# Attention scores kept unscaled in the eviction, the row's step moved into the exponential

## The chip, the cores and the metric

The kernel runs on one core of one Trainium2 chip. The metric is the device time of one execution in microseconds (us). TensorE multiplies matrices into PSUM, VectorE (DVE) and ScalarE (ACT) work element by element, GpSimd (POOL) does casts and issues some DMAs, SyncE (SP) issues the others.

## The reference, cut to what matters

One layer of a perceiver: cross-attention with rounded operands, then self-attention, then a mixture of experts. The change lies in the cross-attention alone. There, 4096 query rows attend to 8192 context rows in 16 heads of 16 channels:

```
q = x @ Wq + bq ; k, v = split(cond @ Wkv + bkv)          # q also times 1/sqrt(16)
q = fq_sym(q, axis=-1)      # s = max|q|/127 per row and head; round(q/s) * s
k = fq_sym(k, axis=-1)
v = fq_sym(v, axis=keys)
attn = softmax(q @ k.T)
attn = fq_unsigned(attn)    # s = max/255 per row; round(attn/s) * s
out = attn @ v
```

The largest entry of a softmax row becomes 255, so the integers of a row are round(exp(s - max(s) + ln 255)), and the row's sum is divided out at the end. A row's score s is the query's step times the product of the query's integers with the key.

## The kernel before, in words

Cross-attention is worked in units. A unit is one tile of 128 query rows of one head against all NK = 8192 keys; there are UNITS = 512 of them. Four units (TG = 4, `t` = 0 to 3) share one head and one load of its keys: I call these four a head; there are HEADS = 128 of them. NM, NE are 5 and 4. Each unit goes through five engines:

- **TensorE** (`scores`, L842 and L845) makes the scores of a unit in five pieces M0 to M4, of 4, 3, 4, 3, 2 PSUM banks of 512 columns (even `t`) or 3, 4, 3, 4, 2 (odd `t`). Pieces go in turn to two PSUM areas, `ring0` and `ring1`. A piece may start when VectorE has evicted the piece two before it. Before the pieces M2 and M4 it repeats two matmuls (L842). The last two pieces listed in a period, N0 and N1, are the first two of the unit after next. `value_product` (AV0, AV1; L857) multiplies the integers of the unit two before with the values; `fold_groups` (L865) folds a finished head's product.
- **VectorE** (`copy_scores`, L918) evicts a piece D0 to D4 from PSUM to the tile `scores` in SBUF, multiplies it by minus the query's step (`step`, one number per row, read from SBUF), and takes the piece's minimum along (`accum_out`, column j of `m_part`). `make_bias` (L925) takes the minimum of the five columns plus ln 255: the exponential's bias. Its place is behind D0 of the next unit.
- **ScalarE** (`exponential`, L977) computes exp(-scores + bias) in four quarters E0 to E3 of 2048, rounded to uint8 in `n_op`, with the sum alongside. It also adds the denominators (DEN, L985), copies a finished head's product out of PSUM (OC, L1001), and scales it (FIN, L995).
- **SyncE** (L721) transposes each quarter by DMA from `n_op` to `pairs`.
- **GpSimd** (`unpack`, L793) casts each quarter to float16 in `nT`, copies steps (L759) and values (L762), and issues the loads of keys (L750) and queries (L752) for the head after next, behind the first cast of `t` = 3.

The order on each engine is written out by hand, one list per engine and unit:

```
PE_STEPS = "M2 M3 AV0 M4 AV1 N0 N1 FOLD".split()
DVE_STEPS = "D0 BIAS D1 D2 D3 INV D4".split()
ACT_STEPS = "DEN E0 FIN E1 OC E2 E3".split()
```

In period u, VectorE evicts unit u + 1 and makes the bias of u; ScalarE works on u; TensorE multiplies the scores of u + 1 and u + 2 and the values of u - 2. INV, DEN and OC come at `t` = 1 alone, for the head before, FOLD too, and FIN at `t` = 2. The value product of a head's first unit (period `t` = 2) waits until FIN has read the head before out of `pO` (`s_fin`). Scores, integers, maxima and bias have two buffers each.

Of the kernel before, what the change touches and what calls it, by code (L numbers as in the profile page):

```python
# [17 lines left out]
P = 128  # L18
# [11 lines left out]
def build(nc, a, out):  # L30
# [27 lines left out]
    with top:  # L58
# [384 lines left out]
        with nc.Block() as block:  # L443
# [98 lines left out]
            def _(dve):  # L542
# [7 lines left out]
                def queries(it):  # L550
                    i = it % 2
                    dve.wait_ge(s_qc, it + 1)
                    link(nc.vector.tensor_reduce(q_amax[:], heads(q_f[i][:]), AX.X, ALU.max, apply_absolute_value=True))
                    link(nc.vector.tensor_scalar(q_st[:], q_amax[:], 1.0 / 127.0, EPS_STEP, ALU.mult, ALU.max))
                    link(nc.vector.tensor_scalar(q_step[:, 0:UNITS].rearrange("p (h t) -> p t h", h=H)
                                                 [:, it * G:(it + 1) * G, :], q_st[:], -1.0, None, ALU.mult))
                    link(nc.vector.reciprocal(q_rst[:], q_st[:]))
                    link(nc.vector.tensor_tensor(heads(q_a[:]), heads(q_f[i][:]), spread(q_rst[:]), ALU.mult))
                    if it >= 2:
                        dve.wait_ge(s_qtp, it - 1)  # L560
                    nc.vector.tensor_scalar(q_int[i][:], q_a[:], ROUND, ROUND, ALU.add, ALU.subtract).then_inc(s_qi, 1)
# [80 lines left out]
        v_op = [sb(f"v_op{i}", [P, KT, 32], F16, xs) for i in range(2)]  # L642
        step = [sb(f"step{i}", [P, TG], F32, xs) for i in range(2)]
        score = [sb(f"scores{i}", [P, NK], F32, xs) for i in range(2)]
# [3 lines left out]
        m_part = [sb(f"m_part{i}", [P, NM], F32, xs) for i in range(2)]  # L648
        m_rest = [sb(f"m_rest{i}", [P, NM], F32, xs) for i in range(2)]
        bias = [sb(f"bias{i}", [P, 1], F32, xs) for i in range(2)]  # L650
        e_sum = [sb(f"e_sum{i}", [P, TG, NE], F32, xs) for i in range(2)]
# [18 lines left out]
        s_mu = sem("scores_copied", xs)  # L670
        s_b = sem("bias_ready", xs)
        s_eu = sem("exp_done", xs)
        s_n = [[sem(f"turned{p}{j}", xs) for j in range(NE)] for p in range(2)]
# [36 lines left out]
        with nc.Block() as block:  # L710
# [36 lines left out]
            def _(pool):  # L747
# [10 lines left out]
                def stage_steps(g, h):  # L758
                    nc.gpsimd.tensor_copy(step[h % 2][:], q_step[:, bass.ds(g * TG + h * QT, TG)]).then_inc(s_st, 1)  # L759

# [150 lines left out]
            def _(dve):  # L911
                def copy_scores(u, j, b, t):
                    at, width = span(t % 2, j)
                    first, last = at // EW, (at + width * BANK - 1) // EW
                    if j == 0 or first < last or at % EW == 0:
                        ge(dve, s_eu, exped(u - 2, last))
                    dve.wait_ge(s_m, scored(u, j))
                    nc.vector.tensor_scalar(score[t % 2][:, at:at + width * BANK], slot(t, j)[:, 0:width * BANK],  # L918
                                            step[b][:, t:t + 1], None, ALU.mult, ALU.min,
                                            accum_out=m_part[t % 2][:, j:j + 1]).then_inc(s_mu, 1)  # L920

                def make_bias(u, par):

                    dve.wait_ge(s_mu, scored(u, NM - 1))
                    nc.vector.tensor_scalar(m_rest[par][:], m_part[par][:], LN255, None, ALU.add, ALU.min,  # L925
                                            accum_out=bias[par][:]).then_inc(s_b, 1)

# [5 lines left out]
                def period(g, h, t):  # L933
# [3 lines left out]
                    for x in DVE_STEPS:  # L937
# [5 lines left out]
                        elif x == "BIAS":  # L943
                            make_bias(u, par)
                        elif t == 1 and exists(i - 1):
                            invert(i - 1)
# [21 lines left out]
            def _(act):  # L968
                def exponential(u, i, hp, t, j):
                    par = t % 2  # L970
# [4 lines left out]
                    if exists(u - 2):  # L975
                        act.wait_ge(s_n[par][j], (u - par) * 8)
                    nc.scalar.activation(n_op[par][:, j * EW:(j + 1) * EW], score[par][:, j * EW:(j + 1) * EW], ACT.Exp,  # L977
                                         bias=bias[par][:], scale=-1.0,
                                         accum_out=e_sum[hp][:, t, j:j + 1]).then_inc(s_eu, 1)
# [23 lines left out]
                def period(g, h, t):  # L1003
                    hp, i = h % 2, g * H + h
                    for x in ACT_STEPS:
                        if x[0] == "E":
                            exponential(i * TG + t, i, hp, t, int(x[1]))
                        elif t == 1 and exists(i - 1) and x == "DEN":
# [693 lines left out]
        s_p = sem("picks_added", mo)  # L1702
        s_out = sem("output_stored", mo)
        for i in range(2):
            sem(f"kept_for_software_queue{i}", mo)
        s_y = [[sem(f"pick_outputs{n}_loaded{b}", mo) for b in range(QT // GB)] for n in range(PICKS)]

# [4 lines left out]
        with nc.Block() as block:  # L1712
            @block.sync
            def _(sp):
# [3 lines left out]
                for n in range(PICKS):  # L1718
                    for b in range(QT // GB):
                        sp.sem_clear(s_y[n][b])  # L1720
                sp.dma_start(gate_sb[:], a["gate"].rearrange("(c p) n -> p c n", p=P)).then_inc(s_gw, 16)
                columns(wg_sb[:], a["up_gate"][:, 0:FS])
# [421 lines left out]
```

## Time and profile before

| | |
|---|---|
| time, median of 3 runs | 6010.56 us (6007.48 to 6025.01) |
| profiled execution | 6010.76 us, of which the profile's span is 6009.2 |
| VectorE busy | 5457.6 us, 91% of the span |
| ScalarE busy | 4786.3 us, 80% |
| GpSimd busy | 4735.2 us, 79% |
| TensorE matmul busy | 4163.2 us, 69% |
| evictions, L918 | 2560, first at 344.5 us, last at 5175.2 |
| exponentials, L977 | 2048, 1997 ns each |

The span is cut by the profiler into lines, engines and waits. A busy share over the whole span mixes the stages; the cross-attention stage is the part from 344 to 5190 us. "Idle before" is the time in which an engine stood before an instruction, with what ended it. A start is when the engine took the instruction; neighbours overlap, so the distance between two starts is what an instruction costs its queue.

### The profile page before, as it was taken

The numbers are of one execution on the slowest core, as the hardware profiler recorded it, in microseconds if no ns is written. First come the engines' busy times: TensorE is split into PE (matmuls) and PEld (weight loads), VectorE is DVE, ScalarE is ACT, GpSimd is POOL, SyncE is SP. The second block draws the span as 40 slices with busy tenths as digits, with TensorE's granted clock in tenths as the row PEclk, the third lists the DMA queues.
The fourth block names the chain that finished last, engine by engine and source line by source line (L and its number), as shares of the span: only waits on it lengthen the run. The fifth ranks groups of instructions, "written<-read, shape, count | busy, mean of one in ns | idle before, by whom it ended". The sixth has DMA issues, their size and how long they took to land. (4 is left out here: it accounts for less than half of the span.)

```text
span 6009.2 us, 141205 instructions
## 1 busy us (share of the span) xinstructions
PE 4163.2 (69%) x48324; PEld 2002.8 (33%) x49040; DVE 5457.6 (91%) x7655; ACT 4786.3 (80%) x6737; POOL 4735.2 (79%) x3414
## 2 busy tenths in 40 slices
PE   7656666666666666666666666666666666679898
PEld 3322222222222222222222222222222222346665
DVE  8889999999999999999999999999999999665444
ACT  5459998999889989998999888988989999546221
POOL 4558898888888888888888888888888888455341
PEclk9889999999999999999999999999999999889899
DMA  4167777777777777777777777777777777540243
GB/s 127 58 130 142 141 142 144 141 141 141 145 138 143 141 144 143 142 142 141 142 137 145 154 140 139 140 143 139 142 138 145 142 142 140 115 73 0 70 140 104
DMA packets 2282499, 783.42 MB, mean 130 GB/s; under 512 B 2189506, under 2 KB 2255909, under 8 KB 2276072
## 3 DMA queue, kind: packets, MB, share of 16 engines
q1 hardware_dynamic: 2239943, 604.79, 49.4%
q0 software_dynamic: 42272, 175.98, 15.5%
q14 instruction: 244, 1.99, 0.1%
q8 instruction: 40, 0.66, 0.1%
HBM read 187.41 MB, written 56.17 MB: 41 GB/s over the span
## 5 line engine op out<-in xcount | busy, mean ns | idle before, releaser
L918 DVE TENSOR_SCALAR_CACHE_REDUCE scores<-ring,step 128x2048 f32<-128x2048 f32 (+2 forms) x2560 | 4780.3, 1920 | 58.4 <-PE ring L845 46.6
L977 ACT ACTIVATE n_op<-scores,bias 128x2048 uint8<-128x2048 f32 x2048 | 4076.3, 1997 | 280.9 <-DVE m_rest L925 280.7
L793 POOL CAST nT<-pairs 128x2048 f16<-128x2048 uint8 x2048 | 3790.9, 1890 | 524.5 <-DMA pairs<-n_op 511.0
L845 PE MATMUL ring<-x_all,q_op 128*128 128x512 bf16 x7746 | 2144.5, 384 | 711.4 <-DVE scores L918 638.3
L845 PEld LDWEIGHTS ring<-x_all,q_op 128*128 128x128 bf16 x8192 | 681.8, 98 | 1861.0 <-DVE scores L918 1189.1
L842 PE MATMUL ring<-x_all,q_op 128*128 128x512 bf16 x1793 | 569.6, 388 | 773.0 <-DVE scores L918 743.0
L857 PE MATMUL pO<-nT,v_op 128*32 128x128 f16 x32768 | 658.1, 223 | 151.4 <-ACT att_g L995 109.2
L857 PEld LDWEIGHTS pO<-nT,v_op 128*32 128x32 f16 x32768 | 480.8, 98 | 599.4 <-issue 512.4
L842 PEld LDWEIGHTS ring<-x_all,q_op 128*128 128x128 bf16 x2048 | 116.7, 97 | 995.6 <-DVE scores L918 978.5
L977 ACT ACTIVATION_READ_ACCUMULATOR n_op<-scores,bias 128x1 f32 x2048 | 395.7, 193 | 0.0
L1001 ACT COPY oT<-pO 128x512 f32<-128x512 f32 x128 | 74.9, 585 | 237.7 <-PE pO L857 237.7
L918 DVE DVE_READ_ACCUMULATOR scores<-ring,step 128x1 f32 x2560 | 213.4, 83 | 0.0
L1401 POOL TENSOR_TENSOR k_bd<-kT,head_mask 128x512 f32<-128x512 f32 x128 | 129.3, 1041 | 90.3 <-ACT kT L1506 90.3
L752 POOL DMA_DIRECT2D q_op<-queries_transposed x384 | 188.7, 496 | 0.9 <-issue 0.6
L1796 POOL DMA_INDIRECT expert_outputs<-ys,token_of x78 | 74.8, 959 | 112.1 <-DVE ys L2043 105.4
L865 PEld LDWEIGHTS pO<-fold,oT 128*128 128x128 f32 x1024 | 135.2, 193 | 19.2 <-ACT oT L1001 1.0
L762 POOL COPY v_op<-v_st 128x1024 f16<-128x1024 f16 x128 | 132.0, 1032 | 10.6 <-DMA v_st<-value_integers 10.6
L1557 DVE TENSOR_REDUCE l_max<-pL 128x16 f32<-128x1024 f32 x32 | 39.2, 1225 | 108.8 <-PE pL L1431 108.8
L756 POOL DMA_DIRECT2D v_st<-value_integers x128 | 72.3, 565 | 75.2 <-POOL v_op L762 74.0
L254 PE MATMUL pKV<-wkv_sb,cT 128*128 128x512 f32 x256 | 125.2, 613 | 0.7
L1782 POOL DMA_INDIRECT expert_slots_in<-z_all,slot_of x64 | 62.2, 971 | 79.5 <-DVE slot_of L1993 60.3
L865 PE MATMUL pO<-fold,oT 128*128 128x16 f32 x1024 | 123.9, 253 | 0.7 <-ACT oT L1001 0.7
(233 smaller groups left out, 3419.8 us busy)
## 6 DMA issues: line engine op xcount, KB each, us to landing
x_all<-keys_transposed POOLq DMA_DIRECT2D x128, 768.0 KB, 8.5
v_st<-value_integers POOLq DMA_DIRECT2D x128, 256.0 KB, 3.5
pairs<-n_op SPq DMA_TRANSPOSE x2048, 2.7
keys_transposed<-kT_s POOLq DMA_DIRECT2D x32, 384.0 KB, 3.3
xs<-expert_slots_in SPq DMA_DIRECT2D x78, 128.5 KB, 2.1
expert_slots_in<-zero_row SPq DMA_DIRECT2D x6, 1664.0 KB, 19.1
cT<-in_ctx_T SPq DMA_DIRECT2D x32, 256.0 KB, 2.7
z_all<-expert_outputs SPq DMA_DIRECT2D x4, 2048.0 KB, 12.0
```

What stands on the lines that cost most here:

```text
L254: mm = nc.tensor.matmul(pKV[i][:, g, :], cT[i][:, c, g * P:(g + 1) * P], wkv_sb[:, c, :], start=False, stop=c == DC - 1)
L752: pool.dma_start(q_op[b][r * HD:(r + 1) * HD, :], qT_d[h * HD:(h + 1) * HD, cols]).then_inc(s_qh[b], 16)
L762: nc.gpsimd.tensor_copy(v_op[b][:, :, 0:HD], v_st[b][:].rearrange("p (k d) -> p k d", d=HD)).then_inc(s_vo, 1)
L793: nc.gpsimd.tensor_copy(nT[par][:, j * EK:(j + 1) * EK, :].rearrange("p (a c) b -> p a c b", c=2), src).then_inc(s_un, 1)
L842: nc.tensor.matmul(slot(t, j)[:, n * BANK:(n + 1) * BANK], q_op[b][:, t * P:(t + 1) * P], k_op[b][:, at + n * BANK:at + (n + 1) * BANK], s ...
L845: mm = nc.tensor.matmul(slot(t, j)[:, n * BANK:(n + 1) * BANK], q_op[b][:, t * P:(t + 1) * P], k_op[b][:, at + n * BANK:at + (n + 1) * BAN ...
L857: mm = nc.tensor.matmul(pO[32 * (n % CG):32 * (n % CG) + 32, t, :], v_op[b][:, n, :], nT[t % 2][:, n, :], start=n < CG, stop=n >= KT - CG)
L865: mm = nc.tensor.matmul(pO[:, t, 0:HD], oT[:, t, :], fold[:], start=True, stop=True)
L918: nc.vector.tensor_scalar(score[t % 2][:, at:at + width * BANK], slot(t, j)[:, 0:width * BANK], step[b][:, t:t + 1], None, ALU.mult, ALU.m ...
L977: nc.scalar.activation(n_op[par][:, j * EW:(j + 1) * EW], score[par][:, j * EW:(j + 1) * EW], ACT.Exp, bias=bias[par][:], scale=-1.0, accu ...
L1001: nc.scalar.copy(oT[:], pO[:]).then_inc(s_oc, 1)
L1401: nc.gpsimd.tensor_tensor(k_bd[i][:, c, b], kT[i][:, c, b * B:(b + 1) * B].unsqueeze(1).to_broadcast([P, HC, B]), head_mask[:].unsqueeze(2 ...
```

## The change

The step is kept positive. VectorE multiplies the scores by the constant 1.0 and takes the maximum alongside. ScalarE's exponential takes the row's step as its scale, beside the bias. The bias, which was one operation (minimum of five columns plus ln 255), is two: the first negates the five maxima and takes their minimum into `m_all`, the second multiplies by the step and adds ln 255. A wait on a new semaphore, `maximum_ready`, stands between the two. The tile `step` gets four buffers instead of two. A semaphore of the last stage is allocated in another place and cleared once.

```
-                                                 [:, it * G:(it + 1) * G, :], q_st[:], -1.0, None, ALU.mult))
+                                                 [:, it * G:(it + 1) * G, :], q_st[:], 1.0, None, ALU.mult))
...
-        step = [sb(f"step{i}", [P, TG], F32, xs) for i in range(2)]
+        step = [sb(f"step{i}", [P, TG], F32, xs) for i in range(4)]
...
+        m_all = [sb(f"m_all{i}", [P, 1], F32, xs) for i in range(2)]
...
+        s_ma = sem("maximum_ready", xs)
...
-                    nc.gpsimd.tensor_copy(step[h % 2][:], q_step[:, bass.ds(g * TG + h * QT, TG)]).then_inc(s_st, 1)
+                    nc.gpsimd.tensor_copy(step[h % 4][:], q_step[:, bass.ds(g * TG + h * QT, TG)]).then_inc(s_st, 1)
...
                     nc.vector.tensor_scalar(score[t % 2][:, at:at + width * BANK], slot(t, j)[:, 0:width * BANK],
-                                            step[b][:, t:t + 1], None, ALU.mult, ALU.min,
+                                            1.0, None, ALU.mult, ALU.max,
                                             accum_out=m_part[t % 2][:, j:j + 1]).then_inc(s_mu, 1)
 
-                def make_bias(u, par):
+                def make_bias(u, par, b, t):
 
                     dve.wait_ge(s_mu, scored(u, NM - 1))
-                    nc.vector.tensor_scalar(m_rest[par][:], m_part[par][:], LN255, None, ALU.add, ALU.min,
-                                            accum_out=bias[par][:]).then_inc(s_b, 1)
+                    nc.vector.tensor_scalar(m_rest[par][:], m_part[par][:], -1.0, None, ALU.mult, ALU.min,
+                                            accum_out=m_all[par][:]).then_inc(s_ma, 1)
+                    dve.wait_ge(s_ma, u + 1)
+                    nc.vector.tensor_scalar(bias[par][:], m_all[par][:], step[b][:, t:t + 1], LN255, ALU.mult,
+                                            ALU.add).then_inc(s_b, 1)
...
                     nc.scalar.activation(n_op[par][:, j * EW:(j + 1) * EW], score[par][:, j * EW:(j + 1) * EW], ACT.Exp,
-                                         bias=bias[par][:], scale=-1.0,
+                                         bias=bias[par][:], scale=step[h % 4][:, t:t + 1],
                                          accum_out=e_sum[hp][:, t, j:j + 1]).then_inc(s_eu, 1)
```

On VectorE, the program around one bias in the main loop (D0 of the next unit, the bias, D1) is, before:

```order
L694 ISA
L917 ISA [waits exp_done]
L918 TENSOR_SCALAR scores,m_part<-ring,step 128x1536 [waits scores_ready]
L925 TENSOR_SCALAR m_rest,bias<-m_part 128x5 [waits scores_copied]
L694 REGISTER_ALU
L917 REGISTER_ALU [waits exp_done]
L918 TENSOR_SCALAR scores,m_part<-ring,step 128x2048 [waits scores_ready]
```

And in the changed kernel, whose lines have moved by a few:

```order
L696 ISA
L919 ISA [waits exp_done]
L920 TENSOR_SCALAR scores,m_part<-ring 128x1536 [waits scores_ready]
L927 TENSOR_SCALAR m_rest,m_all<-m_part 128x5 [waits scores_copied]
L930 TENSOR_SCALAR bias<-m_all,step 128x1 [waits maximum_ready]
L696 REGISTER_ALU
L919 REGISTER_ALU [waits exp_done]
L920 TENSOR_SCALAR scores,m_part<-ring 128x2048 [waits scores_ready]
```

The evictions lose their operand `step`, and a second small operation that waits for the first stands ahead of D1 and of the two register operations that belong to D1's wait. On the other engines the order of the instructions is the same in both.

## Rows read from the trace of the kernel before

**Rows 1.** Busy time by engine, PEclk, DMA share, GB/s, middle of the stage.

```profile
1000.00:5000.00 4000.00, 2690.60 (x35805) 1169.42 (x36387) 3955.25 (x5191) 3597.32 (x4765) 3517.18 (x2438) 0.99 0.74 142
```

**Rows 2.** Waits in 340 to 5210 us: us in total, times, longest.

```profile
POOL nT L793 <- DMA pairs<-n_op: 511.0, 232, 9.8
ACT n_op L977 <- DVE m_rest L925: 280.7, 266, 26.0
ACT oT L1001 <- PE pO L857: 237.7, 128, 12.5
PE pO L857 <- ACT att_g L995: 109.2, 127, 1.3
PEld pO L857 <- POOL nT L793: 86.9, 95, 11.7
DVE scores L918 <- PE ring L845: 46.6, 44, 11.7
PE pO L857 <- POOL nT L793: 42.2, 14, 11.4
```

**Rows 3.** Groups by line and form: busy us, mean ns, idle before (VectorE).

```profile
L918 DVE TENSOR_SCALAR_CACHE_REDUCE scores<-ring,step 128x2048 f32<-128x2048 f32 x1024 | 2404.5, 2348 | 22.4 <-PE ring L845 19.6
...
L918 DVE TENSOR_SCALAR_CACHE_REDUCE scores<-ring,step 128x1024 f32<-128x1024 f32 x512 | 652.4, 1274 | 21.4 <-PE ring L845 21.2
```

**Rows 4.** Timeline from 3011 us, a period with t = 2: start, length.

```profile
3011.08 0.15 DVE L925 TENSOR_SCALAR_CACHE_REDUCE m_rest<-m_part 128x5 f32<-128x5 f32 x1
3011.16 2.35 DVE L918 TENSOR_SCALAR_CACHE_REDUCE scores<-ring,step 128x2048 f32<-128x2048 f32 x1
...
3013.43 1.81 DVE L918 TENSOR_SCALAR_CACHE_REDUCE scores<-ring,step 128x1536 f32<-128x1536 f32 x1
...
3014.58 0.74 ACT L995 ACTIVATE att_g<-pO,rden 128x16 f32<-128x16 f32 x4
...
3015.17 2.35 DVE L918 TENSOR_SCALAR_CACHE_REDUCE scores<-ring,step 128x2048 f32<-128x2048 f32 x1
...
3015.47 0.63 PE L857 MATMUL pO<-nT,v_op 128*32 128x128 f16 x32 [0.86 <-ACT att_g L995]
...
3017.00 0.63 PE L857 MATMUL pO<-nT,v_op 128*32 128x128 f16 x32
...
3017.45 1.28 DVE L918 TENSOR_SCALAR_CACHE_REDUCE scores<-ring,step 128x1024 f32<-128x1024 f32 x1
...
3017.59 1.04 PE L845 MATMUL ring<-x_all,q_op 128*128 128x512 bf16 x4
...
3018.66 2.35 DVE L918 TENSOR_SCALAR_CACHE_REDUCE scores<-ring,step 128x2048 f32<-128x2048 f32 x1
```

**Rows 5.** Timeline of VectorE in the self-attention: an operation from PSUM without scalar operand.

```profile
5385.41 1.22 DVE L1562 TENSOR_TENSOR l_sub<-pL,l_max 128x1024 f32<-128x1024 f32 x1
5386.55 0.41 DVE L1588 TENSOR_TENSOR x_all<-x_all,p_last 128x256 f32<-128x256 f32 x1
```

**Rows 6.** Timeline of VectorE at the end: sixteen operations with one per-row scalar.

```profile
5981.39 6.42 DVE L2052 SCALAR_TENSOR_TENSOR x_all<-z_all,weight,x_all 128x256 f32<-128x256 f32 x16
```

**Rows 7.** Timeline of VectorE in the query stage: each waits for the one before.

```profile
242.86 0.18 DVE L554 TENSOR_SCALAR q_st<-q_amax 128x32 f32<-128x32 f32 x1
243.07 0.20 DVE L555 TENSOR_SCALAR q_step<-q_st 128x32 f32<-128x32 f32 x1
```

**Rows 8.** Timeline of VectorE in the projection, in a register loop.

```profile
5253.43 0.43 DVE L1128 BATCH_NORM_STATS2 stats_ln<-x_all  x1 [0.24 <-DVE x_all L1126]
```

**Rows 9.** Groups by line and form (ScalarE).

```profile
L977 ACT ACTIVATE n_op<-scores,bias 128x2048 uint8<-128x2048 f32 x2048 | 4076.3, 1997 | 280.9 <-DVE m_rest L925 280.7
L985 ACT ACTIVATE den_parts<-e_sum 128x4 f32<-128x4 f32 x512 | 96.3, 189 | 0.0
L1521 ACT ACTIVATE prob<-l_sub,rms_r 128x1024 f32<-128x1024 f32 x32 | 36.8, 1150 | 68.7 <-DVE l_sub L1562 68.7
```

**Rows 10.** DMA issues: count, KB each, median us to landing.

```profile
x_all<-keys_transposed POOLq DMA_DIRECT2D x128, 768.0 KB, 8.5
```

More of the change, by code:

```diff
@@ L943, in period @@
                         elif x == "BIAS":
-                            make_bias(u, par)
+                            make_bias(u, par, h % 4, t)
                         elif t == 1 and exists(i - 1):
@@ L968, in _, with exponential @@
             def _(act):
-                def exponential(u, i, hp, t, j):
+                def exponential(u, i, h, t, j):
+                    hp = h % 2
                     par = t % 2
@@ L1006, in period @@
                         if x[0] == "E":
-                            exponential(i * TG + t, i, hp, t, int(x[1]))
+                            exponential(i * TG + t, i, h, t, int(x[1]))
                         elif t == 1 and exists(i - 1) and x == "DEN":
@@ L1702, in build @@
         s_p = sem("picks_added", mo)
-        s_out = sem("output_stored", mo)
         for i in range(2):
             sem(f"kept_for_software_queue{i}", mo)
+        s_out = sem("output_stored", mo)
         s_y = [[sem(f"pick_outputs{n}_loaded{b}", mo) for b in range(QT // GB)] for n in range(PICKS)]
@@ L1720, in _ @@
                         sp.sem_clear(s_y[n][b])
+                sp.sem_clear(s_out)
                 sp.dma_start(gate_sb[:], a["gate"].rearrange("(c p) n -> p c n", p=P)).then_inc(s_gw, 16)
```

## The prediction

> **What bounds the kernel now.** I read the busy shares of a stretch in the middle of the cross-attention first, then who waits for whom, then the groups by form, then the timeline of one period. VectorE is busy 3955 of 4000 us, ScalarE 3597, GpSimd 3517 [rows 1]. In the whole stage VectorE stands before its evictions for PE only 46.6 us, of which 11.7 are the start [rows 2]. So the stage of some 4830 us runs at VectorE's pace: what its queue loses or gains per unit counts 512 times, what goes by heads 128 times. The others have slack, but little: ScalarE waits 280.7 us for the bias (26.0 of it at the start) and 237.7 us, 1.9 us a head, for the value product before OC [rows 2]. One unit is 4000 us / (5191/12.25) = 9.44 us of wall time: 5191 VectorE instructions in the stretch, 12.25 a unit (5 evictions and 1 bias, each with its accumulator read, and a quarter of an INV).
>
> One place is tight although nothing shows as a wait there, and the timeline of `t` = 2 tells it [rows 4]. FIN ends at 3014.58 + 0.74 = 3015.32. AV0, which waited 0.86 us for it, runs 3015.47 to 3016.10; then M4, then AV1 3017.00 to 3017.63, then N0 at 3017.59 to 3018.63, and VectorE's D0 starts at 3018.66. VectorE had freed N0's PSUM area at 3017.45, 0.14 before N0 started, which is the usual delay. So N0 was held by neither, but TensorE had become free only then: FIN has no reserve left. All 127 later heads show the wait for FIN, 109.2 / 127 = 0.86 us each [rows 2].
>
> **The change part by part.**
>
> *Evictions, 2560, without the per-row scalar.* From start to start, the 2048-wide ones take 2.27 us, the 1536-wide ones 1.74, the 1024-wide one here 1.21 [rows 4]. At 1.0417 ns a column (the slope between the means, (2348 - 1274)/1024 = 1.049, is close [rows 3]) that leaves 0.14 us fixed. What is the fixed part without such a scalar? The operation from PSUM of 1024 columns goes from 5385.41 to 5386.55, 1.14 us: 0.075 fixed [rows 5]. The bias operation, same kind as the eviction, constants only, five columns: 3011.08 to 3011.16, 0.08 [rows 4]. The operations with one such scalar take 6.42/16 = 0.40 us for 256 columns (0.267), so 0.13 fixed [rows 6]. The scalar costs 0.055 to 0.065 us, and I take 0.062 for the wide ones. Per unit that is 5 x 0.062 = 0.31, except that in even periods D4 can't give its share: N0 of four banks (1.04) plus 0.14 plus 0.03 fills D4's 1.21 [rows 4]. Even periods gain 0.25, odd 0.31: 1.12 us a head. Bounds: 0 (the fixed part belongs to the PSUM source) to 0.31 x 4 = 1.24.
>
> *The bias in two operations, 512 times.* Before, it costs the queue 0.08. After: the first is 0.15 long [rows 4], 0.165 with the end of its accumulator read as I take it; the second may start some 0.035 later, as between 242.86 + 0.18 and 243.07 [rows 7]: 0.20. The second has one per-row scalar and one column: 0.13 by rows 6 at least. But the queue could be filled ahead before, and now the wait empties it, with two register operations between the second operation and D1. Where a wait and register work meet, the gap is up to 0.24 [rows 8]. I take 0.20 instead of 0.13. Sum 0.40, which is 0.32 more; bounds 0.25 (0.20 + 0.13 - 0.08) and 0.45 (gap 0.24 for 0.035 and again the 0.13). Queued behind it are D1 and, through the PSUM area, M3 of TensorE; ScalarE's E0 gets its bias 0.25 later. A head: 4 x 0.32 = +1.28.
>
> *So VectorE alone:* 1.28 - 1.12 = +0.16 us a head, x128 = +20 us.
>
> *Exponentials, 2048, with a second per-row operand.* With one per-row operand, the bias, 2048 columns take 1997 ns; the slope is 0.833 (1706), so 291 fixed; with one per-row scale, L1521 has 1150 - 853 = 297; without any, L985 has 189 - 3 = 186 [rows 9]. Either operand alone costs 105. No row has both. Bounds: 0 to 0.21 (twice that); I take 0.095 each. ScalarE has 3597 of 4000 us busy, 8.48 a unit; with 4 x 0.095 it is 8.86, under 9.44: it does not become the bound by its sum, and would only from (9.44 - 8.48)/4 = 0.24 each, or, if OC's 1.9 us a head stay, from 0.12.
>
> The Trainium skill ("ScalarE: Activation LUTs", section "What ACT_TABLE_LOAD costs") states about 93 ns for each per-row pointer operand, and so adds a second like the first. The trace agrees on the first (105 by mean length); by 93 the terms below stand.
>
> *What hides it, and where the cover is gone.* OC starts when AV1 of `t` = 1 ends, which hangs on VectorE's D2; that shifts by the 0.32 less two evictions, +0.20. From OC to the end of FIN there are E2, E3, E0: 3 x 0.095 = +0.285. So FIN ends 0.49 later against VectorE's start of period 1, 0.46 against that of period 2. AV0, M4, AV1 and N0 follow in one piece: D0 starts at 7.58 + 0.46 = 8.04 after the bias instead of 7.58. VectorE's own chain would allow 0.40 + 2.21 + 1.68 + 2.21 = 6.50 for the end of D3, plus 0.14 + 1.03 + 0.03 for N0: 7.70. So 0.34 us a head are lost to a new wait of D0 for PE: x128 = +44 us. Bounds: 0 (ScalarE's second operand free; then FIN is 0.18 later and N0 just fits) and 0.70 x 128 = 90 (0.21 each).
>
> *The transposes behind the key load.* E3 of `t` = 3 ends 0.86 us later than now against VectorE: seven more exponentials and the FIN above, less the stall of D0. Its transpose is issued around the time at which the 768 KB of keys start, which take 8.5 us [rows 10]; GpSimd's 511 us of waiting for transposes and TensorE's 86.9 + 42.2 = 129 us for its casts come from there, and of these 46.6 reach VectorE, 36% [rows 2]. At that share 0.86 us more would be 0.31 a head; some of the heads are already late, so I take 0.25: +32 us. Bounds 0 and 0.86 x 128 = 110.
>
> *The rest.* Four `step` buffers, the sign, one more semaphore clear of the last stage: once or unchanged in count, nothing against 0.3%.
>
> Sum: 20 + 44 + 32 = +96 us on the profiled execution's 6010.8, 6107. The profiled execution is within 0.2 us of the median of the runs, so I keep it.
>
> **The rivals.**
>
> *A. VectorE's own sum decides and is a gain.* The pair of bias operations costs only 0.25 more, D4 gives its share too, and ScalarE's second operand is hidden, so FIN stays. For it: overlap of neighbours is everywhere, and VectorE alone is the busiest. Against: the tight N0. Place: D1 right behind the pair. 0.25 - 0.31 = -0.06 a unit: 512 x 0.06 = 31 us less, 5980. It decides if the pair adds less than 0.28 and an exponential gains under 0.03.
>
> *B. The two cancel.* VectorE as forecast or a little better, FIN's delay small, the transposes still hidden: -15 to +20 us, 5996 to 6030.
>
> *C. The eviction keeps its fixed part.* Then VectorE's sum is +0.32 x 512 = 164 us: 6175, and FIN has cover again, because D3 ends later too. The row against it is the 1.14 us of an operation that also reads PSUM [rows 5]. The Trainium skill ("VectorE: DVE Perf Modes", section on the TRN2 errata) gives 120 cycles fixed from PSUM and 58 from SBUF; by that rule the evictions' 0.14 is PSUM's and nothing is saved. Rows 5 contradict it as far as start to start goes.
>
> *D. ScalarE or the transposes become the bound.* With 0.15 or more an exponential ScalarE's 8.48 + 0.6 a unit and OC's wait leave nothing, and E3 of `t` = 3 falls wholly behind the keys: 90 + 110 + 20 = 220 us at the bounds, half of it likely: 6120 to 6200.
>
> **How the numbers follow.** Forecast 0.50 (6060 to 6130); A 0.12; B 0.18; C 0.08; D 0.12. The predicted time is the forecast's 6107, drawn slightly toward the smaller transposes term: 6095. A measurement of this kernel tells 0.3%, 18 us, from no change. Faster is A and a tenth of B and the forecast's edge: 0.14. Same is most of B: 0.14. Slower 0.72. The range leaves out most of A below and the tail of C and D above: 5992 to 6170.
>
> **What would show it.** Evictions of 2048 columns at about 2.29 us mean and 2.21 from start to start (2.35 would be C); the second bias operation about 0.2 us long, D1 0.40 after the first one's start (0.33: A); exponentials at 2.09 us (2.00: A or B; over 2.15: D); VectorE's wait for PE risen from 46.6 to about 100 us or more, before the first eviction of a unit, with AV0's wait for FIN over 1 us; TensorE's waits for casts above 129 us. The prediction is wrong if VectorE's idle time stays at 50 us, or if the exponentials' length doesn't move.

## The result, and the profile after

The changed kernel takes 6116.59 us, median of 4 runs (6102.07 to 6124.31), beside 6011.16 us (6007.48 to 6025.01, 4 runs) for the kernel before: ratio 1.0173, 95% interval 1.0155 to 1.0191, so 105 us slower. The forecast was 6095, in a range of 5992 to 6170. The profiled execution is the fastest of the four, 6102.07 us with a span of 6100.6, so the two traces are 91.4 us apart (6009.2 before), and the working below goes by that distance. Each trace here is of one execution, and that can lie off its kernel's median: those of e2, e7 and e10 lie 21 to 27 us above it, those of the changed kernel and of e12 15 and 12 us below.

The same stretch as in [rows 1], same columns. VectorE's busy time fell although the kernel got slower, ScalarE's rose, the granted clock fell from 0.99 to 0.97:

```profile
1000.00:5000.00 4000.00, 2657.47 (x35124) 1159.71 (x35695) 3888.82 (x5502) 3684.36 (x4673) 3457.51 (x2395) 0.97 0.78 139
```

The groups by line and form (busy us, mean ns | idle before) answer to [rows 3, 9]:

```profile
L983 ACT ACTIVATE n_op<-scores,bias,step 128x2048 uint8<-128x2048 f32 x2048 | 4265.7, 2089 | 233.4 <-DVE bias L930 233.4
...
L920 DVE TENSOR_SCALAR_CACHE_REDUCE scores<-ring 128x2048 f32<-128x2048 f32 x1024 | 2343.2, 2288 | 79.3 <-PE ring L847 76.6 <-issue 0.2
...
L920 DVE TENSOR_SCALAR_CACHE_REDUCE scores<-ring 128x1024 f32<-128x1024 f32 x512 | 621.7, 1214 | 38.0 <-PE ring L847 37.1
...
L930 DVE TENSOR_SCALAR bias<-m_all,step 128x1 f32<-128x1 f32 x512 | 109.6, 214 | 18.3
```

An eviction is 60 ns shorter at both widths, an exponential 92 ns longer, and the new second bias operation stands idle 18.3 us before its 512 starts. The waits in the stage, 340 to 5300 us, beside [rows 2]:

```profile
POOL nT L795 <- DMA pairs<-n_op: 576.1, 241, 9.8
...
DVE scores L920 <- PE ring L847: 114.3, 215, 11.2
PE pO L859 <- ACT att_g L1001: 114.1, 126, 1.3
...
PEld pO L859 <- POOL nT L795: 66.6, 100, 11.3
...
PE pO L859 <- POOL nT L795: 23.2, 7, 11.0
```

VectorE's wait for TensorE rose from 46.6 us in 44 places to 114.3 in 215; GpSimd's for the transposes from 511 to 576 us; TensorE's for the casts fell (66.6, and 23.2 at its matmuls, beside 86.9 and 42.2). The timeline has the two kinds of place that the prediction spoke of, the end of a `t` = 2 period (from 3036 us) and the bias pair of the loop (from 3001.9 us):

```profile
3001.88 2.29 DVE L920 TENSOR_SCALAR_CACHE_REDUCE scores<-ring 128x2048 f32<-128x2048 f32 x1 [0.27 <-PE ring L847]
...
3004.09 0.15 DVE L927 TENSOR_SCALAR_CACHE_REDUCE m_rest<-m_part 128x5 f32<-128x5 f32 x1
...
3004.29 0.21 DVE L930 TENSOR_SCALAR bias<-m_all,step 128x1 f32<-128x1 f32 x1
...
3004.50 1.76 DVE L920 TENSOR_SCALAR_CACHE_REDUCE scores<-ring 128x1536 f32<-128x1536 f32 x1
...
3036.54 0.63 PE L859 MATMUL pO<-nT,v_op 128*32 128x128 f16 x32 [1.04 <-ACT att_g L1001]
...
3038.21 1.22 DVE L920 TENSOR_SCALAR_CACHE_REDUCE scores<-ring 128x1024 f32<-128x1024 f32 x1
...
3039.71 2.29 DVE L920 TENSOR_SCALAR_CACHE_REDUCE scores<-ring 128x2048 f32<-128x2048 f32 x1 [0.28 <-PE ring L847]
```

From the first bias operation to D1 it is 0.41 us here (0.08 before); AV0 waits 1.04 us for FIN (0.86 before), and D0 behind it waits 0.28 where it waited for nothing.

**A measure for the rest.** One VectorE bias operation per unit (L925, now L927) is a clock mark in every trace. The distance from one to the next, by the position `t` from which it starts, over the units 64 to 447 (96 heads), has nearly the same value each time; its median is what the instructions take in the normal case. What the mean has above the median comes from single heads. I call the sum of the four medians the fixed length of a head and the difference to the mean its excess. A late cast, below, is a cast of the integers that TensorE has to wait for; a late head is one whose period at `t` = 1 lasts over 0.3 us more than the median.

```
us from bias op to bias op, median (mean)
          t=0            t=1           t=2             t=3           head
before    9.86 (9.92)    8.83 (9.06)   9.85 (9.98)     8.77 (8.86)   37.3 (37.8)
after     9.94 (10.02)   8.86 (8.88)   10.23 (10.74)   8.80 (8.92)   37.8 (38.6)
```

The fixed length grew by 0.08 + 0.03 + 0.38 + 0.03 = 0.52 us, times 128 heads 67 us. The excess grew from 0.51 to 0.74, 29 us. Together 96, beside the spans' 91.4. The excess also moved: at `t` = 1, where late casts of the integers cause it, it went from 0.23 to 0.02 (6 late heads of 96 before, 1 now); at `t` = 2 from 0.13 to 0.51.

What happens at `t` = 2 is in the clock. First the timeline of a period in which it fell, with one row from 3037.55 us for comparison, where it had not; then the busy shares before, in and after the fall (columns as in [rows 1]):

```profile
3037.55 0.59 PE L847 MATMUL ring<-x_all,q_op 128*128 128x512 bf16 x2
...
3302.03 1.04 PE L847 MATMUL ring<-x_all,q_op 128*128 128x512 bf16 x4 [1.37 <-DVE scores L920]
...
3304.11 0.83 PE L859 MATMUL pO<-nT,v_op 128*32 128x128 f16 x32 [1.05 <-ACT att_g L1001]
...
3305.70 1.06 PE L847 MATMUL ring<-x_all,q_op 128*128 128x512 bf16 x2
...
3306.69 1.04 PE L859 MATMUL pO<-nT,v_op 128*32 128x128 f16 x32
...
3306.80 1.23 DVE L920 TENSOR_SCALAR_CACHE_REDUCE scores<-ring 128x1024 f32<-128x1024 f32 x1 [0.94 <-PE ring L847]
...
3308.80 2.29 DVE L920 TENSOR_SCALAR_CACHE_REDUCE scores<-ring 128x2048 f32<-128x2048 f32 x1 [0.76 <-PE ring L847]
```

```profile
3300.00:3304.30 4.30, 1.89 (x23) 0.62 (x23) 4.30 (x5) 4.30 (x9) 4.30 (x4) 1.00 0.73 124
3304.40:3307.70 3.30, 2.97 (x63) 1.52 (x51) 2.36 (x3) 3.30 (x3) 3.30 (x3) 0.50 0.50 97
3307.90:3310.00 2.10, 1.50 (x7) 0.49 (x5) 1.34 (x3) 2.10 (x4) 1.49 (x3) 1.00 0.67 129
```

TensorE was busy 1.89 of 4.30 us, waiting first for VectorE and then for FIN, and then was busy 2.97 of 3.30 us at a granted 0.50 (1.2 GHz). Two of its 512-column matmuls took 1.06 us instead of 0.59, and VectorE waited 0.94 and 0.76 us. I count a stretch at a granted 0.50 as one fall; at the edges of the stage one more or less hangs on where it is cut. In the whole stage the clock fell 62 times for 229 us in all (25 times for 99 us before), and 55 of the falls began in a period of `t` = 2 (8 before). The falls are the whole excess there: over the same 96 heads the 45 periods of `t` = 2 with a fall last 11.32 us in the mean, the 51 without one 10.23, which is the median. Before, it was 11.37 (8) and 9.86 (88). So a fall costs such a period about 1.1 us here.

### The profile page after: what moved, and what is told of

It is laid out like the page before. It is cut to its first block and busy times, and to the rows that moved or that the text cites. A ratio compares the mean times of both kernels' runs of the same rounds, so it can differ in the third digit from the quotient of the medians.

```text
span 6100.6 us, 141718 instructions
## 1 busy us (share of the span) xinstructions
PE 4187.9 (69%) x48324; PEld 2020.1 (33%) x49040; DVE 5461.3 (90%) x8167; ACT 4978.4 (82%) x6737; POOL 4744.5 (78%) x3414
## 3 DMA queue, kind: packets, MB, share of 16 engines
q1 hardware_dynamic: 2239943, 604.79, 53.8%
q0 software_dynamic: 42272, 175.98, 14.7%
## 5 line engine op out<-in xcount | busy, mean ns | idle before, releaser
L920 DVE TENSOR_SCALAR_CACHE_REDUCE scores<-ring 128x2048 f32<-128x2048 f32 (+2 forms) x2560 | 4643.7, 1860 | 129.4 <-PE ring L847 114.3
L983 ACT ACTIVATE n_op<-scores,bias,step 128x2048 uint8<-128x2048 f32 x2048 | 4265.7, 2089 | 233.4 <-DVE bias L930 233.4
L859 PE MATMUL pO<-nT,v_op 128*32 128x128 f16 x32768 | 678.9, 227 | 137.4 <-ACT att_g L1001 114.1
L859 PEld LDWEIGHTS pO<-nT,v_op 128*32 128x32 f16 x32768 | 496.6, 100 | 602.4 <-issue 535.9
L983 ACT ACTIVATION_READ_ACCUMULATOR n_op<-scores,bias,step 128x1 f32 x2048 | 394.7, 193 | 0.0
L1007 ACT COPY oT<-pO 128x512 f32<-128x512 f32 x128 | 75.0, 586 | 186.0 <-PE pO L859 186.0
L920 DVE DVE_READ_ACCUMULATOR scores<-ring 128x1 f32 x2560 | 212.7, 83 | 0.0
L930 DVE TENSOR_SCALAR bias<-m_all,step 128x1 f32<-128x1 f32 x512 | 109.6, 214 | 18.3
```

Source lines behind the costliest of these rows:

```text
L859: mm = nc.tensor.matmul(pO[32 * (n % CG):32 * (n % CG) + 32, t, :], v_op[b][:, n, :], nT[t % 2][:, n, :], start=n < CG, stop=n >= KT - CG)
```

## The experiments

Ratios are to runs of the kernel before on the same chip, with their 95% interval. The experiments ran in three groups, each on another chip; the kernel before had medians of 6009.3 to 6016.3 us beside them, so two versions are told apart by their ratios, and times of different groups only to some 5 us. "Fixed" and "mean" are a head's lengths as above; "falls" counts falls of the granted clock in the stage; "casts" adds TensorE's and its weight loads' waits for the casts; "transposes" is the median from issue to landing.

```
kernel                                ratio (95% interval)     fixed  mean   falls (at t=2)  casts us  transposes us
before                                1                        37.3   37.8   25 (8)          129       2.7
after                                 1.0173 (1.0155, 1.0191)  37.8   38.6   62 (55)         90        3.1
e1  evictions by a constant           0.9910 (0.9880, 0.9941)  36.6   37.4   58 (47)         104       2.7
e2  exponentials with row scale       1.0062 (1.0038, 1.0085)  37.5   38.4   28 (11)         177       3.1
e3  bias pair alone                   1.0282 (1.0255, 1.0309)  38.6   39.2   61 (43)         45        2.7
e4  after, FIN first                  1.0064 (1.0035, 1.0093)  37.5   38.1   25 (3)          163       3.1
e5  before, FIN first                 0.9978 (0.9967, 0.9988)  37.3   37.8   26 (0)          144       2.7
e6  after, two more matmuls           1.0144 (1.0108, 1.0179)  37.8   38.4   46 (14)         141       3.1
e7  after, registers first            1.0078 (1.0051, 1.0106)  37.6   38.4   34 (15)         180       3.1
e8  e7 and FIN first                  1.0048 (1.0033, 1.0062)  37.2   38.0   44 (3)          174       3.1
e9  after, FIN first, keys late       1.0041 (1.0018, 1.0064)  37.5   38.0   21 (10)         124       3.1
e10 e8 and keys late                  1.0017 (1.0000, 1.0034)  37.2   38.0   44 (14)         144       3.1
e11 e9, second op behind D1           1.0017 (0.9993, 1.0040)  36.7   37.7   29 (23)         201       3.1
e12 before, FIN first, keys late      0.9961 (0.9946, 0.9975)  37.3   37.5   23 (0)          103       2.7
```

**e1, the evictions alone.** The kernel before with the row's scalar replaced by a constant. It leaves the query's step out of the scores, so its output is not the reference's; it is there for its time.

```
-    step[b][:, t:t + 1], None, ALU.mult, ALU.min,
+    -1.0, None, ALU.mult, ALU.min,
```

> Kernel before with one part of the change alone: the evictions multiply by the constant -1.0 and no longer by the row's step, which is left out of the computation. Bias and exponential as before. Theory (the per-row scalar costs 0.06 us an eviction, FIN has no reserve): periods of t = 0, 1, 3 shrink by 0.26 to 0.31 us each, that of t = 2 grows by about 0.1 instead of shrinking, because FIN and what TensorE does behind it don't come earlier and D0 now waits for PE: -0.76 us a head, -97 us, about 5914. If FIN doesn't matter: -1.12 a head, -143 us, 5868. If the fixed part of an eviction belongs to its PSUM source: 0, mean of the 2048-wide evictions unchanged at 2348 ns.

5964.98 us, 51 less than the kernel before beside it; 97 were forecast. The length answers [rows 3]:

```profile
L918 DVE TENSOR_SCALAR_CACHE_REDUCE scores<-ring 128x2048 f32<-128x2048 f32 x1024 | 2342.2, 2287 | 74.9 <-PE ring L845 71.2 <-ACT n_op L977 0.9
```

The 61 ns are the whole price of the scalar. The medians fell by 0.25, 0.30 and 0.30 at `t` = 0, 1 and 3, but rose by 0.11 at `t` = 2 instead of falling by 0.25: the wait behind FIN (0.35) comes up as soon as VectorE gets faster, without any change on ScalarE. Fixed length -0.74 a head. The mean fell by only 0.44, since the clock now falls 58 times. So two fifths of what the evictions give is taken back, which my number had left out.

**e2, the exponentials alone.** Scale from a tile that holds -1 everywhere (its allocation and its fill are cut here); the values are the same.

```
-    bias=bias[par][:], scale=-1.0,
+    bias=bias[par][:], scale=negs[:, t:t + 1],
```

> Kernel before with the exponential's scale read per row from a tile that holds -1.0, all else as before. Theory: exponentials 2.09 us long instead of 2.00; FIN ends 0.285 us later, D0 after t = 2 waits for PE about 0.3 a head: +36 us, and some 25 more from short falls of TensorE's clock or late transposes: 6045 to 6075. Rival (ScalarE has slack for it, nothing hangs on FIN): 6011.

6061.24 us, in the range expected. The waits for casts:

```profile
PEld pO L859 <- POOL nT L795: 102.9, 67, 10.7
PE pO L859 <- POOL nT L795: 74.5, 20, 10.4
```

The fixed length grew by 0.25, all at `t` = 2 (9.85 to 10.10): FIN's delay with VectorE untouched. The excess grew by 0.37 in this trace, most of it at `t` = 1 (0.23 to 0.53, 11 late heads), where TensorE waited 177 us for casts instead of 129. The trace's execution lies 21 us above the median: between the medians the excess is worth 13 us, 0.1 a head. So the third term of the prediction does show at its place here, with its size uncertain.

**e3, the bias pair alone.** The added operation multiplies by ones; the last stage's semaphore clear is in it too (cut here, with the new tile and semaphore).

```
-    nc.vector.tensor_scalar(m_rest[par][:], m_part[par][:], LN255, None, ALU.add, ALU.min,
-                            accum_out=bias[par][:]).then_inc(s_b, 1)
+    nc.vector.tensor_scalar(m_rest[par][:], m_part[par][:], 1.0, None, ALU.mult, ALU.min,
+                            accum_out=m_all[par][:]).then_inc(s_ma, 1)
+    dve.wait_ge(s_ma, u + 1)
+    nc.vector.tensor_scalar(bias[par][:], m_all[par][:], ones[:, 0:1], LN255, ALU.mult, ALU.add)
```

> Kernel before with the bias made in two operations, the second with one per-row scalar (a column of ones), as in the changed kernel. Theory: D1 starts 0.40 us after the first instead of 0.08 in the loop, where two register operations stand between, and 0.33 in the unrolled first and last 16 heads; 384 x 0.32 + 128 x 0.25 = +155 us, less what FIN and the transposes gain as cover: 6140 to 6168. Rival (the waits behind the bias have slack and absorb most of it): under 6060.

6189.64 us, over the 6140 to 6168 expected. All four medians rose by 0.32 to 0.34, 1.32 a head, 169 us of the 173 between the medians. The forecast's 0.32 a unit stands; the cover for FIN and the transposes is there, and the late casts are gone, but the falls of the clock rose to 61.

The three fixed parts add up to the change: evictions -1.10 (four periods, without the wait behind FIN), pair +1.32, and in the changed kernel 0.29 for that wait, +0.51 of the 0.52. The ratios don't add up (-0.9, +0.6 and +2.8% make 2.5, not 1.7), mostly because e1 and e2 each pay for the wait behind FIN, 0.35 and 0.25 a head against 0.29 once in the changed kernel, and e3 has cover for it: AV0's wait for FIN is 68.1 us in its trace, against 109.2 before. What is left lies in the excess.

**e4, FIN ahead of the exponential.** In the changed kernel.

```
-    ACT_STEPS = "DEN E0 FIN E1 OC E2 E3".split()
+    ACT_STEPS = "DEN FIN E0 E1 OC E2 E3".split()
```

> Changed kernel with FIN moved ahead of E0 in ScalarE's list. Theory (FIN's delay is what costs at t = 2): TensorE's wait for FIN of 114 us goes, D0 waits no longer, -0.34 us a head, -43 us: 6073; if the falls of TensorE's clock in that period, at which some heads have 1 us more, come from that wait of PE as well, another -50: 6023. Rival (the delay lies with transposes behind the key load): within 15 us of the changed kernel, 6100 to 6120.

6047.61 us, between the forecast's 6073 and 6023 and 69 us faster than the changed kernel (66 by the ratios). The waits, as [rows 2]:

```profile
PEld pO L859 <- POOL nT L795: 99.1, 85, 10.4
...
DVE scores L920 <- PE ring L847: 67.7, 51, 11.1
PE pO L859 <- POOL nT L795: 63.7, 18, 10.1
```

TensorE's wait for FIN is gone, and the median at `t` = 2 is 9.94, as at `t` = 0: the wait behind FIN was 10.23 - 9.94 = 0.29 us a head, 37 us. The rest of the gain is clock: of 55 falls at `t` = 2 three are left. But the late casts are back at `t` = 1 (excess 0.02 to 0.32, 6 late heads).

**e5, the same order in the kernel before.**

> Kernel before with FIN moved ahead of E0 in ScalarE's list. Theory: before had no stall from FIN, only no reserve, so the fixed length of a head (37.3 us) stays; of the 0.13 us a head that t = 2 lost to late FINs some goes: 0 to -15 us. If it gains as the changed kernel did (about -65), FIN did cost before too and my reading of the timeline was wrong.

6000.37 us, all four medians as before. So FIN cost nothing there, as the prediction read it from [rows 4]; only the excess at `t` = 2 (0.13) is gone.

**e6, more work for TensorE.** Two matmuls of M3 are made twice in the periods that start at `t` = 2, in the pause before the falls.

```
-    if j == NM - 1 or j == NM - 3:
+    if j == NM - 1 or j == NM - 3 or (j == NM - 2 and t == 3):
```

> Changed kernel, two matmuls of the piece M3 repeated in the period of t = 2 (results are the same), so that TensorE stands less before the value product that waits for FIN. The falls of TensorE's granted clock in the trace (62 stretches of the stage against 25 before) come at t = 2, and periods of t = 2 have a mean of 10.74 us against a median of 10.23. Theory (idle TensorE ahead of the falls brings them): falls back to about 25, mean of t = 2 near 10.25, -50 to -60 us: about 6060. Rival (the falls only accompany late transposes, or come in any case): no change, 6116, and the extra 0.43 us of matmuls may delay D3 a little.

6096.39 us: 20 us less than the changed kernel, not the 57 expected, and the two ratios' intervals overlap, so the time alone doesn't show a gain. The trace shows the rest. The falls at `t` = 2 went from 55 to 14 and its mean from 10.74 to 10.33, 0.41 a head, with the median unchanged; that shows that TensorE's pause brings the falls and that they cost what the mean has above the median. But 0.27 of the 0.41 came back, at `t` = 1 (8.88 to 9.07, late casts, 6 late heads instead of 1) and `t` = 0 (10.02 to 10.10, 19 falls instead of 5). The wait behind FIN is as long as in the changed kernel (median 10.23), which points to the falls, and not to that wait, as what had kept the late casts away.

**e7, the register work ahead of the pair.** D1 waits for an exponential of two units ago, a wait that needs two register operations on VectorE; they stood between the second bias operation and D1. Here D1's wait is placed ahead of the pair (shortened, with a comment added).

```
 elif x == "BIAS":
+    if exists(u + 1):
+        free_scores(u + 1, 1, t1)     # D1's wait for the exponential, taken from copy_scores
     make_bias(u, par, h % 4, t)
```

> Changed kernel, D1's wait for the exponential moved ahead of the two bias operations, and with it the two register operations that stand between the second bias operation and D1. Theory: D1 starts 0.33 us after the first bias operation in the loop too, as it does in the unrolled heads (0.13 behind the second instead of 0.21). 384 units x 0.08 = -30 us, of which t = 2 gives nothing as long as it waits for FIN: about -23, 6093. Rival (0.21 is the length of the second operation, whatever stands behind it): no change.

```profile
2991.81 0.15 DVE L931 TENSOR_SCALAR_CACHE_REDUCE m_rest<-m_part 128x5 f32<-128x5 f32 x1
...
2992.00 0.21 DVE L934 TENSOR_SCALAR bias<-m_all,step 128x1 f32<-128x1 f32 x1
2992.14 2.28 DVE L924 TENSOR_SCALAR_CACHE_REDUCE scores<-ring 128x2048 f32<-128x2048 f32 x1
```

From the second operation to D1 it is 0.14 us instead of 0.21, and the medians fell by 0.08 or 0.09 at `t` = 0, 1 and 3. At `t` = 2 nothing fell, as expected, since the wait behind FIN sets it. The time, 6063.95, is 29 us better than expected. The profiled execution (span 6089.3) is 27 us above that, so its excess is above what is typical, and where the further gain sits was not seen. In it only 15 falls are left at `t` = 2, and there are 10 late heads (excess at `t` = 1 0.50), though the wait behind FIN is as before.

**e8 and e10, both additions undone, and the keys late.** FIN first and registers first; in e10, as in e9 and e12, the loads of the next keys and queries are issued after the last cast of `t` = 3 instead of after the first (comments added):

```
-    if t == 3 and exists(u + 2 * TG):      # ahead of the casts
-        keys(g + (h + 2) // H, (h + 2) % H, i + 2)
+    (the same two lines behind the last cast)
```

> The changed kernel with two of its additions undone: D1's wait for the exponential before last stands ahead of the bias pair (so that the pair and D1 follow each other without register work between), and FIN stands ahead of E0 in ScalarE's order. By the theory that a head's fixed length is the sum of VectorE's operations: 37.54 us with FIN first, less 3 x .08 for the registers = 37.2 to 37.3 (medians 9.86, 8.78, 9.86, 8.71), .1 to .2 under the kernel before. Excess by clock falls and late casts .4 to .6 a head, as in the other runs. 6015, between 5995 and 6035. Rival (the two gains are one and the same, given back as clock falls): not under the one with registers first alone at 6050 or the one with FIN first at 6048.

> The same with the key and query loads issued after the last cast of t = 3. The theory: fixed length as in the run above (37.2), and the late casts at t = 1 (some .3 a head on the mean) go, while clock falls at t = 2 come back by .1 to .2: 6000, between 5985 and 6020. Rival (the loads are harmless, the excess only moves): the same as the run above within .3%.

6038.63 and 6018.71 us. The fixed length came out as expected, 37.2, under the 37.3 of the kernel before. The time of e8 lies above its range (to 6035), that of e10 just inside its own (to 6020); the excess is 0.75 and 0.76, the latter in an execution 26 us above the median. The clock falls 44 times, now 28 and 30 of them at `t` = 0, and in e10 the excess at `t` = 1 is zero but at `t` = 2 it is 0.43.

**e9, e4 with the keys late.**

> Changed kernel with FIN first (as in e4) and the loads of keys and queries issued behind the last cast of t = 3 instead of behind the first, so that the last transpose of t = 3 is not under way together with them. Theory (the 0.32 us a head that e4 still loses at t = 1 come from that transpose): mean of t = 1 falls from 9.18 to near its median of 8.86, TensorE's 163 us of waiting for casts nearly go, -40 us against e4: about 6005. Rival (the next head's transposes suffer as much): 6030 to 6050.

6036.07 us. The excess at `t` = 1 went from 0.32 to 0.00, as the theory had it, but at `t` = 2 it rose from 0.05 to 0.30, and the time lies in the rival's 6030 to 6050; from e4 it is not told apart. All of the 0.30 comes from six heads whose period at `t` = 2 lasts 14.7 us in the mean. In five of them TensorE waits over 1 us for casts, now those of the unit of `t` = 0, the next behind the moved loads. So in e9 to e11 the excess at `t` = 2 is mostly late casts, with a fall of the clock behind them, and not the falls behind FIN.

**e11, the second operation behind D1.** On top of e9, so that neither of VectorE's operations waits for the one just issued.

```
-    DVE_STEPS = "D0 BIAS D1 D2 D3 INV D4".split()
+    DVE_STEPS = "D0 MAX D1 BIAS D2 D3 INV D4".split()
```

> The changed kernel with FIN first, key loads late, and the second bias operation put behind D1: nothing then waits at VectorE between the first bias operation, D1 and the second. Theory (VectorE's order of issue is the whole price): the pair costs its two operations without the two starts that wait on a result just written, some .12 to .28 less per unit: fixed 36.7 to 37.2 a head, time 5950 to 5990. ScalarE's first exponential of each period starts about 2.2 us later by D1. Rival (ScalarE's start is what counts: E3 and so the casts and transposes come 2.2 us later, and TensorE waits for them at t = 1 and t = 2): 6040 or more, with ScalarE's waits for the bias and TensorE's for the casts grown.

```profile
3004.71 2.29 DVE L920 TENSOR_SCALAR_CACHE_REDUCE scores<-ring 128x2048 f32<-128x2048 f32 x1
...
3006.92 0.21 DVE L932 TENSOR_SCALAR bias<-m_all,step 128x1 f32<-128x1 f32 x1
3007.05 1.75 DVE L920 TENSOR_SCALAR_CACHE_REDUCE scores<-ring 128x1536 f32<-128x1536 f32 x1
```

The second operation costs 0.13 us and no more; the fixed length is 36.7, 0.6 under the kernel before. Yet the time is 6016.18, not told apart from the kernel before, nor clearly from e9. ScalarE starts each unit later (its waits for the bias are 319.5 us, beside 170.8 in e9), its last transposes land late, and then TensorE and VectorE stop:

```profile
2777.13 9.23 POOL L795 CAST nT<-pairs 128x2048 f16<-128x2048 uint8 x5 [11.56 <-DMA pairs<-n_op]
...
2782.93 1.04 PE L859 MATMUL pO<-nT,v_op 128*32 128x128 f16 x32 [6.56 <-POOL nT L795]
...
2785.83 1.23 DVE L920 TENSOR_SCALAR_CACHE_REDUCE scores<-ring 128x1024 f32<-128x1024 f32 x1 [6.55 <-PE ring L847]
```

TensorE's waits for casts are 163.5 + 37.7 = 201 us, the most of all kernels, and the mean at `t` = 2 is 10.55 against a median of 9.73. The rival had this mechanism, but its 6040 was too high, as the theory's 5990 was too low.

**e12, the two orders without the change.**

> The kernel before with FIN first and the key and query loads late: what these two orders are worth without the change. Fixed length as before (37.3 a head), the mean at t = 1 down from 9.06 to about 8.86: 5985, between 5970 and 6000. If the late loads only move the excess to other periods: 6000, as with FIN first alone.

5987.78 us, ratio 0.9961: the mean at `t` = 1 is its median, 8.83, and at `t` = 2 9.86. VectorE's wait for TensorE, beside 46.6 us in [rows 2]:

```profile
DVE scores L918 <- PE ring L845: 17.8, 30, 11.2
```

Of these 17.8 us, 11.2 us are the start. This version is faster than both kernels; of the versions with the whole change none is faster than the kernel before. With the best orders found on either side (e12 against e10 or e11) the change still costs 0.6%.

## Why the prediction came out right

**VectorE's evictions.** Forecast 0.062 us less each, measured 0.060 (2348 to 2288, 1274 to 1214). The choice of [rows 5] as the nearest row was right: the fixed part of 0.14 us was the scalar's by nearly half, and rival C falls with it. The Trainium skill ("VectorE: DVE Perf Modes", section on the TRN2 errata) gives 120 cycles fixed from PSUM, by which nothing would be saved; the trace does not agree: start to start D0 takes 4.09 - 1.88 = 2.21 us, 0.08 over 2048 columns at the forecast's 1.0417 ns, and it did save the 0.06.

**The pair.** Forecast 0.32 more a unit, measured 0.33 (e3). Its parts: the dependent start 18.3/512 = 0.036 us; the second operation to D1 0.21. The row is now known too: it is 0.13 for the operation, as [rows 6] had it, and 0.08 for register work behind a wait (e7, e11). With the evictions that makes VectorE's own sum +0.23 a head (37.54 in e4, where FIN's wait is gone, less 37.31), 29 us, forecast 20. Rival A's price for the pair, 0.25 more, isn't that of the changed kernel; it is that of e7, e8 and e10, and e11 is cheaper still, but not even with FIN out of the way do e8, e10 and e11 fall below the kernel before, let alone to 5980.

**ScalarE.** Forecast 0.095 an exponential, measured 0.092. The Trainium skill's 93 ns for each per-row pointer operand ("ScalarE: Activation LUTs", section "What ACT_TABLE_LOAD costs") agrees with the trace for the second operand as well. ScalarE did not become the bound: 3684 of 4000 us busy.

**FIN and the wait behind it.** Forecast 0.34 us a head and 44 us; measured 0.29 and 37 (e4). The prediction found it in a place where the profile before shows no wait, by setting two rows of the timeline side by side, and e5 confirms that it lost nothing, e1 and e2 that it had no reserve. The sign "over 1 us" for AV0's wait was too high on average: 114.1/126 = 0.91.

**The transposes behind the key load.** Here the step was wrong, though its size wasn't. It said: 0.25 a head through late casts, visible as TensorE's waits for casts above 129 us. Those waits fell to 90 us, and the excess at `t` = 1 nearly vanished. In its place came 0.38 a head at `t` = 2 from falls of the clock, net +0.23 with the other periods, or 29 us beside the 32 forecast.

The delay itself came about as forecast, with the stall of D0 taken off it: over the same 96 heads E3 of `t` = 3 ends 8.91 us behind its unit's bias operation in the median, 8.19 before, 0.72 later. (The forecast's own terms, 7 x 0.095 + 0.46 - 0.34, give 0.79 and not 0.86.) The unit's last cast follows, 20.46 us behind that operation instead of 19.72. What failed is the rule that turned this delay into lost time, a fixed share of 36%. The median cast is in time in both kernels; the time is lost in the few late heads, by several microseconds each, and their number doesn't follow the delay: e7 has its E3 at 8.92 and its last cast at 20.55, as good as the changed kernel's, and 10 late heads where that has 1. (The 36% also had the 11.7 us of the stage's start in it.)

In these traces it goes with the falls. The three kernels with 43 falls or more at `t` = 2 (the changed one, e1, e3) have 0 to 4 late heads; the other seven with the key loads in their old place have at most 15 such falls and 6 to 11 late heads, e2 and e7 with the wait behind FIN among them. e6 took the falls away, left that wait, and the late heads came back. That the falls would rise was in no term and in no rival. How a fall at `t` = 2 keeps casts from being late was not found.

Summed: 29 + 37 + 29 = 95 us, forecast 20 + 44 + 32 = 96. The agreement of the total is luck in part: two of three terms stand by their mechanism, the third is a loss of another kind that happened to have its size. Rival B would have needed FIN in time, rival D an exponential of 2.15 us or more and OC's wait used up; OC still waits 186.0 us.

Of the 105 us between the medians, 91 to 96 are so accounted for; the rest lies within what the runs of one kernel differ (22 us for the changed one).

**What stays open.** Why the excess trades places is shown only in its pattern: the removal of one cause (FIN, late casts, falls at `t` = 2) mostly let another grow, between 0.2 (e12) and 1.0 us a head (e11). The numbers of late heads are small ones of a single trace per kernel. What decides between 0.2 and 0.8 for a given fixed length wasn't isolated.

## What to carry to other kernels

Price an edit on the bound engine by start-to-start distances in the timeline, not by mean lengths, and separate the fixed length of a period (median) from its excess (mean less median): the fixed part followed the sum of VectorE's operations and the wait behind FIN in every experiment to within a tenth of a microsecond, the time didn't. A gain on the bound engine of a tightly coupled loop can be taken back by what is next in line (e1 lost two fifths of its own), so remove first the tight wait (here FIN), which cost one word moved in a list of steps. A dependent pair of tiny operations can be split around a long one, which took 0.2 us off each unit here (e11); but see who waits for its result, since the time did not follow. And a mean delay doesn't price a wait that only a few late cases cause: count those.

## What the runs showed of the hardware that was not expected

- **The transposes get slower with a per-row scale on ScalarE.** In all nine kernels whose exponential takes the scale from a tile, the transposing DMAs take 3.1 us to land, in the five others 2.7 (medians). The same bytes are moved, and in e2 even the same values. The rows are the queue's share and the issues, first of the kernel before, then of e2:

```profile
q1 hardware_dynamic: 2239943, 604.79, 49.4%
...
pairs<-n_op SPq DMA_TRANSPOSE x2048, 2.7
```

```profile
q1 hardware_dynamic: 2239943, 604.79, 54.8%
...
pairs<-n_op SPq DMA_TRANSPOSE x2048, 3.1
```

  The packets took 54.8% of 16 engines' span instead of 49.4%. Neither a longer unit (e3, 47.4%) nor a shorter one (e1, 49.7%) does this; the nine lie between 53.8 and 55.5%. Why is open.
- **Register operations behind a wait cost VectorE 0.08 us a unit,** though before the change, without a wait ahead of them, they cost nothing that shows: 0.21 from the second operation to D1 in the loop, 0.13 where the same code stands unrolled with constants:

```profile
357.56 0.21 DVE L930 TENSOR_SCALAR bias<-m_all,step 128x1 f32<-128x1 f32 x1
357.69 2.28 DVE L920 TENSOR_SCALAR_CACHE_REDUCE scores<-ring 128x2048 f32<-128x2048 f32 x1
```

- **TensorE's clock falls in a kernel where TensorE is not the bound can cost as much as a wait.** A period with a fall is 1.1 us longer, there are 62 falls instead of 25, and e4 and e6 show that a wait of some tenths of a microsecond for another engine, or the pause of TensorE that it adds to, at one place of the period, decides whether they come there.
